# One program from the last scan on: 59 expert tiles in one pipeline, W1 fetched for each tile, W2 of all experts resident

## The reference, cut to what matters

```python
h = _layernorm(x) * (1 + ca) + sa                 # per sequence: modulation from c
xi, z = split(rmsnorm(h) @ W_in)                  # 512 channels each
xc = silu(causal_conv4(xi));  dt, B, C = split(xc @ W_x);  dt = softplus(dt @ W_dt + b_dt)
h_t = exp(dt * A) * h_(t-1) + dt * xc * B         # scan over 512 tokens, 16 states a channel
y = (sum over states of h_t * C + D_skip * xc) * silu(z)
x = x + ga * (h + y @ W_out)
h = _layernorm(x) * (1 + cb) + sb                 # then the experts
w, idx = top_k(h @ Wg, 2);  w = softmax(w)        # 8 experts, 2 for a token
e_out = relu((xhat * gamma_e + beta_e) @ W1_e + b1_e) @ W2_e + b2_e + h
x = x + gb * sum over the two experts of w * e_out
```

## Time and profile before

| | us |
|---|---|
| time, median of 3 runs (1747.89 to 1760.78) | 1750.55 |
| the profiled execution, its own time | 1749.44 |
| its span, first to last instruction | 1747.5 |
| PE busy | 1357.7 (78%) |
| DVE busy | 1205.2 (69%) |
| POOL busy | 1048.7 (60%) |
| ACT busy | 907.9 (52%) |

### The profile page before, as it was taken

The page is one execution under the profiler, slowest core; times in us unless marked ns, Lnnn a source line. Parts: engine busy times, 40 slices in busy tenths (PEclk is TensorE's granted clock), DMA queues, the critical chain, the costliest instruction groups (busy, mean ns, idle before and its releaser), DMA issues. The chain is left out here.

```text
span 1747.5 us, 26223 instructions
## 1 busy us (share of the span) xinstructions
PE 1357.7 (78%) x7968; PEld 1102.1 (63%) x7969; DVE 1205.2 (69%) x2076; ACT 907.9 (52%) x1514; POOL 1048.7 (60%) x938
## 2 busy tenths in 40 slices
PE   4667677777787777877877786878862999999994
PEld 1344555555566565565655556766752899999994
DVE  3788998998887878879688786784201555555552
ACT  3677677677657757767575674663321222222220
POOL 2576877987796895987698588784441222222221
PEclk8789888798788899889899988989986999999997
DMA  6222212311331442432333135536565752222224
GB/s 217 62 60 71 52 47 71 104 52 47 106 121 52 137 140 67 130 115 70 101 101 114 48 108 167 149 112 182 169 194 185 230 159 55 54 56 54 56 57 111
DMA packets 129518, 182.67 MB, mean 105 GB/s; under 512 B 19428, under 2 KB 84471, under 8 KB 129159
## 3 DMA queue, kind: packets, MB, share of 16 engines
q1 hardware_dynamic: 103494, 133.86, 25.6%
q0 software_dynamic: 16064, 28.53, 6.7%
q10 hardware_dynamic: 9856, 19.05, 3.8%
HBM read 144.04 MB, written 41.54 MB: 106 GB/s over the span
## 5 line engine op out<-in xcount | busy, mean ns | idle before, releaser
L742 POOL TENSOR_TENSOR dBu<-u,brep 128x512 f32<-128x512 f32 x512 | 644.0, 1329 | 72.4 <-DVE hs L1745 61.9
L1745 DVE TENSOR_TENSOR_SCAN hs<-psum,dBu 128x512 f32<-128x512 f32 x512 | 609.2, 1209 | 86.9 <-ACT psum L960 61.9
L960 ACT ACTIVATE psum<-dt,aneg 128x512 f32<-128x512 f32 x512 | 346.7, 690 | 175.6 <-DVE hs L1745 170.7
L1312 PE MATMUL psum<-ident,hs 128*128 128x128 f32 x2048 | 314.1, 303 | 141.5 <-DVE y L1756 99.9
L1312 PEld LDWEIGHTS psum<-ident,hs 128*128 128x128 f32 x2048 | 257.3, 156 | 220.2 <-DVE y L1756 145.6
L2027 POOL DMA_INDIRECT sum_d<-ysb_late,token x52 | 80.9, 1556 | 329.2 <-DVE ysb_late L2149 320.0
L2045 ACT ACTIVATE w_now<-w_sb 128x2048 f32 x52 | 99.1, 1910 | 299.4 <-issue 249.1
L944 ACT ACTIVATE hc<-psum,ct 128x512 f32<-128x512 f32 x256 | 174.4, 681 | 150.4 <-PE psum L1312 143.7
L1321 PE MATMUL psum<-ident,hc 128*128 128x128 f32 x1024 | 179.5, 306 | 76.6 <-DVE gT L1765 39.5
L1321 PEld LDWEIGHTS psum<-ident,hc 128*128 128x128 f32 x1024 | 136.8, 159 | 116.0 <-ACT hc L944 60.6
L1756 DVE SCALAR_TENSOR_TENSOR y<-psum,ct,y 128x512 f32<-128x512 f32 x240 | 175.0, 729 | 47.2 <-PE psum L1312 45.7
(11 more groups left out here) (242 smaller groups left out, 1739.2 us busy)
## 6 DMA issues: line engine op xcount, KB each, us to landing
brep<-b_d SPq DMA_DIRECT2D x128, 256.0 KB, 3.3
expert_pieces<-in_W SPq DMA_DIRECT2D x52, 512.0 KB
w_sb<-in_W SPq DMA_DIRECT2D x16, 1024.0 KB
xg_late<-rows_d ACTq DMA_DIRECT2D x52, 257.0 KB, 2.8
dt<-in_W SPq DMA_DIRECT2D x12, 512.0 KB, 5.7
u<-in_W SPq DMA_DIRECT2D x12, 512.0 KB, 5.2
h_d<-hmod SPq DMA_DIRECT2D x8, 512.0 KB, 2.9
hres<-h_d SPq DMA_DIRECT2D x8, 512.0 KB, 5.6
```

The costliest lines, as they stand in the source:

```text
L742: nc.gpsimd.tensor_tensor(dBu[:, i % RING, :], u[:, p, c, :], brep[:, s % 4, :], ALU.mult).then_inc(s_dBu, 1)
L960: nc.scalar.activation(dA[:, i % DA_RING, :], dt[:, p, c, :], ACT.Exp, scale=aneg[:, c, s:s + 1]).then_inc(s_dA, 1)
L1312: last = nc.tensor.transpose(T[:, i // DT, c * P:(c + 1) * P], hs[:, s % 2, c, i * P:(i + 1) * P], ident[:, :])
L1745: nc.vector.tensor_tensor_scan(hs[:, s % 2, c, :], dA[:, i % DA_RING, :], dBu[:, (n * UNITS + i) % RING, :], 0.0, ALU.mult, ALU.add).then_ ...
```

## The change

The constants: the second part of the table now has 32 tiles (9 to 40) and the third 30. From tile 12 (`BEGIN`) on, all 59 tiles run in one pipeline of the form of stage C, but in the same program, without the barrier, written out tile by tile. It begins inside the last step of the last sequence. W2 of all experts (and all of b1, b2, gamma, beta) lies in SBUF: `w2_sb` takes the place of `dt`, `u`, `hs`, and one half of `xc` and `sz`, so expert `e`'s W2 is loaded when what lies at `home(e)` is dead. Experts 0 to 3 are loaded in sequence 7 at steps 5 and 9, experts 5, 4, 6, 7 after the last scan. W1 is no longer resident and no longer copied by ACT: SP fetches 1 MB for each tile into one of two buffers (`late_w1`), for tile `t + 2` once the first product of tile `t` is done. The chain of sequence 7 is spread over tiles 14 to 31. Tiles 8 to 11 keep their old form, with a ring of 5 slots, and their hidden tile lies in `xnT` and `hmod` and no longer in `xc` and `sz`, so ACT's wait for `s_gate` (the gating of sequence 6, on POOL) is gone there.

```diff
-TA = 19
-TF = 2 * NTOK // P + E - 1 - TA
-TABLES = ((0, 9), (9, TA - 9), (TA, TF))
+BEGIN = 12
+TILES = 2 * NTOK // P + E - 1
+TABLES = ((0, 9), (9, 32), (41, TILES - 41))
+XR, YR = 5, 4
...
+        w2_sb = sb("w2_sb", [P, E, FC, D])
+
+        def home(e):
+            return w2_sb[:, e, :, :].rearrange("p k d -> p (k d)").rearrange("p (c l) -> p c l", l=L)
+
+        dt, u = [home(0), home(4)], [home(1), home(5)]
+        hs = [home(6), home(7)]
+        xc = [home(2), sb("xc1", [P, CH, L])]
+        sz = [home(3), sb("sz1", [P, CH, L])]
...
-        hT_late = [t[:, 0, 0:2, :].rearrange("p c (f t) -> p (c f) t", t=P) for t in (xc, sz)]
-        xg_of = [xg0[:, :], xc[:, 0, 2:4, :].rearrange("p c l -> p (c l)")[:, 0:XW]]
+        hT_late = [xnT[:, :, :].rearrange("p c (f t) -> p (c f) t", t=P), hmod[:, :, :].rearrange("p i (f t) -> p (i f) t", t=P)]
+        xg_of = [xg0[:, :], modp_flat[:, 0:XW]]
...
+        xgl_of = [xg0[:, :], dflat[:, 0:XW], dflat[:, XW:2 * XW], modp_flat[:, 0:XW], dflat[:, 2 * XW:3 * XW]]
+        ysl = dflat[:, 3 * XW:3 * XW + YR * D].rearrange("p (r d) -> p r d", d=D)
...
-            return g % 3 if g < 4 * LATE else (g - 4 * LATE) % 7
+            return g % 3 if g < 4 * LATE else (g - 4 * LATE) % 5
...
                     if slot_of(g) >= 3:
-                        sp.wait_ge(s_dBu, (NB - 1) * UNITS)
-                        sp.wait_ge(s_dA, (NB - 1) * UNITS)
+                        sp.wait_ge(s_zp, NB * CH)
...
+            def late_rows(t):
+
+                i = t - BEGIN
+                sp.wait_ge(s_tab, 2 if t < TABLES[2][0] else 3)
+                sp.wait_ge(s_sc, 16 * (2 * TI * 6 if t < TABLES[2][0] else 2 * TI * NB + E + 1))
+                if i >= XR:
+                    sp.wait_ge(s_yin, t - XR + 1)
+                elif i % XR == 0:
+                    sp.wait_ge(s_yin, BEGIN - 1)
+                elif i % XR == 3:
+                    sp.wait_ge(s_yin, BEGIN)
+                else:
+                    sp.wait_ge(s_scan, NB * UNITS)
+                row = sp.value_load(tab[0:1, 1, t:t + 1], min_val=0, max_val=E * EROWS)
+                sp.dma_start(xgl(t), rows_d[bass.ds(row, P), :]).then_inc(s_cx[i % XR], 16)
...
+            def late_w1(t):
+                if t < BEGIN + 2:
+                    for g in range(4 * BEGIN - 5, 4 * BEGIN):
+                        if (slot_of(g) >= 3) == (t == BEGIN) and slot_of(g) != 2:
+                            sp.wait_ge(*piece_read(g))
+                else:
+                    sp.wait_ge(s_thp, 2 * (t - 2) + 2)
+                e = expert_of(t)
+                sp.dma_start(w1_of[t % 2], W1[bass.ds(e, 1), :, :].rearrange("a (k p) f -> p (a k) f", p=P)).then_inc(s_w1[t % 2], 16)
+
+            def all_w2(e):
+                sp.dma_start(w2_sb[:, e, :, :], W2[e].rearrange("(k p) d -> p k d", p=P)).then_inc(s_we, 16)
...
+                    if n == 7 and s == 5:
+                        sp.wait_ge(s_dA, n * UNITS)
+                        all_w2(0)
+                        sp.wait_ge(s_dBu, n * UNITS)
+                        all_w2(1)
+                        sp.dma_start(gam[:, :], gamma).then_inc(s_small, 16)
+                        sp.dma_start(bet[:, :], beta).then_inc(s_small, 16)
+                        sp.dma_start(b1_sb[:, :], b1).then_inc(s_small, 16)
+                    if n == 7 and s == 9:
+                        sp.wait_ge(s_g, n * CH)
+                        all_w2(2)
+                        sp.wait_ge(s_gate, n * CH)
+                        all_w2(3)
...
-                for t in range(LATE + 4, LATE + 6):
-                    tile_rows(t)
-                    tile_pieces(t, range(4))
-                load_gate(NB - 1)
-                for t in range(LATE + 6, TA):
-                    tile_rows(t)
-                    tile_pieces(t, range(4))
-                store_base(NB - 1)
-                sp.wait_ge(s_bast, 16 * NB)
-                sp.wait_ge(s_sc, 16 * (2 * TI * NB + E + 1))
-                sp.wait_ge(s_st, 16 * TA)
-                sp.wait_ge(s_tab, 3)
+                first_columns(BEGIN)
+                late_rows(BEGIN)
+                late_w1(BEGIN)
+                sp.wait_ge(s_dBu, NB * UNITS)
+                all_w2(5)
+                sp.dma_start(b2_sb, b2.to_broadcast([P, E * D])).then_inc(s_b2, 16)
+                sp.wait_ge(s_dA, NB * UNITS)
+                all_w2(4)
+                late_rows(BEGIN + 1)
+                late_w1(BEGIN + 1)
+                sp.wait_ge(s_tr, NB * UNITS)
+                all_w2(6)
+                all_w2(7)
+                for t in range(BEGIN + 2, BEGIN + XR):
+                    late_rows(t)
+                for t in range(BEGIN, TILES):
+                    if t + 2 < TILES:
+                        late_w1(t + 2)
+                    if t > BEGIN and t - 1 + XR < TILES:
+                        late_rows(t - 1 + XR)
+                sp.wait_ge(s_st, 16 * TILES)
+                for n in range(0, NB, 2):
+                    store_out(sp, n)
...
+                tile_out(BEGIN - 1)
+                gate(NB - 1, 1)
                 send_rows(NB - 2, 1)
...
+                for t in range(BEGIN, TILES):
+                    late_out(t)
+                    if t == 16:
+                        ln2(NB - 1)
...
-                if t in (LATE, LATE + 1):
-                    act.wait_ge(s_gate, (NB - 1) * CH)
+                if t == LATE + 1:
+                    act.wait_ge(s_hst, 16 * NB)
...
+            def late_x(t):
+                i = t - BEGIN
...
+                elif i < 4:
+                    pe.wait_ge(s_g, NB * CH)
+                else:
+                    pe.wait_ge(s_yb, i - 3)
+                for k in range(DC):
+                    last = nc.tensor.transpose(xl(t)[:, k, :], xgl(t)[:, k * P:(k + 1) * P], ident[:, :])
+                last.then_inc(s_txp, 1)
...
+            def first(t):
+                i = t - BEGIN
+                pe.wait_ge(s_txt, t + 1)
+                pe.wait_ge(s_w1[t % 2], 16 * (i // 2 + 1))
+                if i == 0:
+                    pe.wait_ge(s_scan, NB * UNITS)
+                elif i == 1:
+                    pe.wait_ge(s_hc, 2 * NS * NB)
+                else:
+                    pe.wait_ge(s_th, 2 * (t - 2) + 2)
+                for f in range(FC):
+                    for k in range(DC):
+                        last = nc.tensor.matmul(hl(t)[:, f, :], w1_of[t % 2][:, k, f * P:(f + 1) * P], xgT_of[t % 2][:, k, :],
+                                                start=(k == 0), stop=(k == DC - 1))
...
+            def second(t):
+                e = expert_on(pe, t)
+                if t == BEGIN:
+                    pe.wait_ge(s_we, 16 * E)
+                pe.wait_ge(s_th, 2 * t + 2)
+                if t + 2 < TILES:
+                    pe.wait_ge(s_txt, t + 3)
+                if t < BEGIN + 2:
+                    pe.wait_ge(s_g, NB * CH)
+                else:
+                    pe.wait_ge(s_yb, t - BEGIN - 1)
+                for k in range(FC):
+                    last = nc.tensor.matmul(PS[:, 6 + t % 2, 0:D], hT_late[t % 2][:, k, :],
+                                            w2_sb[:, bass.ds(e, 1), k, :].rearrange("p a d -> p (a d)"),
+                                            start=(k == 0), stop=(k == FC - 1))
...
                         tile_y(LATE + 3, 1)
+                        late_x(BEGIN)
                     states(n, s, 1)
                     states(n, s, 3)
+                    if n == 7 and s == 15:
+                        first(BEGIN)
...
+                late_x(BEGIN + 1)
+                pe.wait_ge(s_txt, BEGIN + 1)
                 y_t(NB - 1)
+                first(BEGIN + 1)
+                late_x(BEGIN + 2)
+                second(BEGIN)
+                for t in range(BEGIN + 2, TILES):
+                    if t + 1 < TILES:
+                        late_x(t + 1)
+                    first(t)
+                    second(t - 1)
+                    if t in (14, 16):
+                        out_proj(NB - 1, NB, t - 14)
+                        out_proj(NB - 1, NB, t - 13)
+                    if t == 20:
+                        pe.wait_ge(s_opr, 2 * NB)
+                        xf_t(NB - 1)
+                    if t == 22:
+                        scores(NB - 1)
+                    if t == 24:
+                        pe.wait_ge(s_scr, NB)
+                        counts(NB - 1)
+                    if t == 26:
+                        rank(2, OB)
+                    if t == 29:
+                        pe.wait_ge(s_cnt, NB)
+                        table(2, XB)
+                second(TILES - 1)
...
-            def step(j, r, begins):
-                e = expert(act, j)
-                act.wait_ge(s_we, 32 * (e + 1))
-                after(act, s_hp, j - 1)
-                nc.scalar.activation(w1_now[:, r % 2, :, :], w1_sb[:, bass.ds(e * DC, DC), :], ACT.Copy).then_inc(s_w1, 1)
...
+            def epilogue():
+                tile_yin(BEGIN - 1)
```

(26 more changed lines are left out.)

547 lines of the change are left out of this document (189 added, 358 removed).

## The result

The changed kernel takes **1691.5 us** (median of 4 runs, 1683.1 to 1697.4) and the kernel before 1750.0 (median of 4, 1747.9 to 1760.8): a ratio of 0.9653, 95% interval 0.9612 to 0.9693, 58 us less. The forecast was 1695, 1674 to 1722.

What follows compares the result with a forecast made beforehand. PE bounds the last stage, and some 80 us before it PE waits. Tile 14's W1 at 1227 + 2.1 + 416.4 + 19 + 5 = 1669.5; + 22.9 + 1.9 = 1694.3; median 1.1 above: 1695 us, range 1674 to 1722.

Steps and rivals of the forecast that it cites:

- 416.4: PE's remaining work from tile 14's first product on: 57 first products, 58 second products and 56 turns, 416.4 us.
- The chain's term: Sequence 7's chain on PE, 11 groups: 19 us added, 17 to 20.
- Before the last scan: Sequences up to the last scan: net -3 us, ends -5 and +10.
- the -4: Sequence 6, tile 8: ACT's relu no longer waits for POOL's gating, and most of that gain stays, -4 us.
- the +1 for loads and selection: Before the last scan: larger selection of part 2, smaller ring of pieces and W2 loads in steps 5 and 9, +1 us.
- Rival D: Sequence 7, steps 5 to 12: late brep or pieces delay the scans, +10 in place of -3, 1708 us; chance 0.10.
- Start: Behind the last scan: 10.75 MB at 320 GB/s, 33.6 us, put tile 14's W1 at 1227; low clock adds 2.1.
- Stalls by DVE: Pipeline: DVE's chain pieces over 1.2 us of room stall PE by 5 us, 0 to 12.
- The fetch of W1 costs nothing: Pipeline: each W1 load took 5.7 us in stage C and has 9.9 us here, so it costs nothing.
- rivals B and E: Pipeline: B, adds fall behind, 1722 us, chance 0.08; E, W1 lands too late in every tile, 1783 us, chance 0.04.
- Rival C: Written-out pipeline: 27 instruction loads at 1.78 us each cost 48 us, 1743 us, no change; chance 0.03.
- The tail: From the last product's end to the end of the span: as before, 22.9 us.

Runs made afterwards that it cites:

- experiment 3: Changed kernel with ACT's wait for POOL's gating put back before the relu of tiles 8 and 9; the scan waits 4.44 us for ACT, against 3.87 for GpSimd without it.
- experiment 4: Changed kernel without the loads of W2 of experts 0 to 3 in sequence 7; 1689.8 us, ratio 0.9680 to the kernel before.
- v_three: Changed kernel with DVE's residual at tile 18, padding one a tile, sequence 6's sends behind tile 14's add; last scan's start to tile 14's first product 33.5 us.
- e_light: Changed kernel without W2 of experts 4 to 7 and all but one row of b2; last scan's start to tile 14's first product 23.2 us, from 32.0.
- e_block: Changed kernel with sequence 7's chain in one block, behind tile 15 on PE and DVE, tile 14 on POOL; gives back 34 us of the 58.
- e_twice: Changed kernel with each W1 fetched twice from tile 18 on and PE waiting for both; 19 us more.

## Why the prediction was right, and where its terms were off

The step that carries the forecast was right: the last stage is bound by PE, it comes earlier, and what PE has left is 7.25 a tile with the chain on top. From tile 14's first product to the last product's end I had 442.5 (416.4 + 2.1 + 19 + 5) and the trace has 438.7: 416.4, about 16 of chain, 5.9 of stalls and what they do to the clock, and the rest rounding. The chain's term was 3 too large: the two products that fill the last part of the table took 3.1 us before and take 1.2 here, with 30 columns in place of 52, and the groups overlap their neighbours by more than the 1 I allowed.

*Before the last scan*: forecast -3, measured +5.3 in this trace. The term was wrong in its mechanism. I took most of the 4.19 us for gained, and noted in the same sentence that GpSimd makes no `dBu` in 5.49 us of gating; that is the wait that took its place (experiment 3, 3.87 for 4.44). So the -4 was 0. Of the 5.3, 3.9 lie ahead of sequence 7, within the spread from execution to execution; 1.4 lie inside it, 0.6 in the first steps, and the W2 loads can account for the rest (experiment 4), so the +1 for loads and selection was about right. Rival D, late loads for the scans, is there at 1 to 2 us and not at 10.

*Start*: forecast 36.5 from the last scan's end to tile 14's product (1190.5 to 1227), measured 30.8 (1198.8 to 1229.6). Off was the rate. I took 320 GB/s; these two windows of the backlog are of the changed kernel:

```profile
1205.00:1210.00 5.00, 4.96 (x30) 4.99 (x31) 0.00 (x0) 0.00 (x0) 0.61 (x1) 0.66 1.06 383
1220.00:1225.00 5.00, 4.24 (x24) 3.81 (x23) 1.33 (x6) 0.00 (x0) 4.25 (x5) 0.72 1.09 370
```

At 375 the 10.75 MB are 28.7 us in place of 33.6, 4.9 less. The 1.05 MB of sends do not belong in the sum at all (v_three). That the time of 1227 came near (1229.6) was luck: the last scan was 8.3 later than forecast, and the start behind it 5.7 shorter. The mechanism was also off. I let tile 14's W1, the last load, set the start. In the trace PE goes from tile 12's second product at 1225.79 to tile 14's first without a wait, and what it waited for last was tile 14's rows and DVE's scaling of them (0.29 and 1.26 us), a little earlier in the same backlog; W1's last landing on record is at 1229.1, half a microsecond ahead. The amount of loads does move the start (e_light, 8.8 of 13.6), but through the rows as well as through W1. The low clock added 1.7 and 2.6 us to the first products of tiles 12 and 13 and nothing to tile 14's, where I had put 2.1; e_block, with tile 12's at 3.81, still has S to F at 32.6, so most of it lay beside waiting.

*Stalls by DVE*: forecast 0.2 + 2.0 + 0.6 + 2.2 = 5. The 2.0 for the residual with statistics came (1.91), and 1.8 more since the product behind it ran at the lower clock (5.40), in the first trace; in the second the same product took 3.72. The 2.2 for top-2 was 0.53: its instructions took from 1318.09 to 1319.9, 1.8 us and not the 3.4 that I read out of the groups of the earlier trace rows, of which one, at 1.3 for a single instruction, took 0.14 here. The 1.55 at 1385 was in no term. That the sum of 5 met 5.9 is in part luck.

*The fetch of W1 costs nothing, rivals B and E*: right. e_twice gives the margin: one W1 more a tile, and the engines are full. The Trainium skill, DMA: Bandwidth & Descriptors, Queues, rings and completion order, has each DMA engine take turns between the queues that have work. By that rule the adds would slow down beside W1 and not stop. The trace agrees: DVE waited for one in 56 tiles. *Rival C*: there are 18 loads of instructions more on the queue shown, and PE stands still three times and not at every load. Each gap stands beside a late step of DVE; two of these are its own work, the third (1385) has no cause that a run shows. The Trainium skill, Runtime: NRT & Kernel Launch, Instruction fetch mechanics, has the crossing to a next block mostly hidden, and this trace agrees but for what is open at 1385. *The tail*: forecast 22.9, measured 22.2.
